# TensorE's program of the second attention, steps 24 to 55, as a loop of eight steps a turn

## The reference, cut to what matters

```python
x = x + tanh(g_xattn[0]) * attention0(layernorm(x), ctx)     # 8 heads of 64
x = x + tanh(g_ffn[0])   * experts(layernorm(x))             # 16 experts, the best 2 of each row
x = x + tanh(g_xattn[1]) * attention1(layernorm(x), ctx)     # 16 heads of 8
x = x + tanh(g_ffn[1])   * fp8_matmul(layernorm(x))
# attention1(q, c): Q = q@Wq+bq; K = c@Wk+bk; V = c@Wv+bv; softmax(Q K^T / sqrt(8)) V @ Wo + bo, by head
```

## Time and profile before

| | |
|---|---|
| time, median of 3 runs | 1152.83 us (1152.71 to 1156.85) |
| the profiled execution's time | 1153.63 us |
| its span, first to last instruction | 1151.9 us |
| PE, DVE, ACT, POOL busy | 90%, 71%, 51%, 56% of the span |
| stage C, VectorE's first to last instruction | 708.5 to 1149.5 us |
| mean granted clock of TensorE | 0.952 |

### The profile page before, as it was taken

How to read it: one execution, slowest core, us unless ns; L and a number is a source line. 1 busy time by engine, 2 the same in 40 slices (tenths; PEclk the granted TensorE clock), 3 DMA queues, 4 the chain that set the end, 5 groups by cost and what they waited for, 6 DMA issues and landing times. The chain is left out here.

```text
span 1151.9 us, 40516 instructions
## 1 busy us (share of the span) xinstructions
PE 1035.9 (90%) x13498; PEld 844.1 (73%) x13498; DVE 814.5 (71%) x2572; ACT 590.3 (51%) x1415; POOL 650.7 (56%) x1155
## 2 busy tenths in 40 slices
PE   4999999996999997499949996888999999899993
PEld 3787878774777775288848985666788888788882
DVE  1777777776777775655525555577899999799984
ACT  2666666662666564144515442234556555465554
POOL 1333333232777777566663545447777777577656
PEclk9999999997999999599979998799999999899997
DMA  3412112331334300144424543111111111111101
GB/s 76 90 42 52 42 38 61 91 75 40 92 95 108 98 25 27 55 139 140 134 74 130 144 137 89 30 30 29 32 38 37 32 37 38 30 37 34 33 24 31
DMA packets 106902, 74.39 MB, mean 65 GB/s; under 512 B 21360, under 2 KB 98288, under 8 KB 106736
## 3 DMA queue, kind: packets, MB, share of 16 engines
q1 hardware_dynamic: 98544, 55.40, 18.5%
q0 software_dynamic: 8192, 16.79, 4.9%
HBM read 38.60 MB, written 33.55 MB: 63 GB/s over the span
## 5 line engine op out<-in xcount | busy, mean ns | idle before, releaser
L678 ACT ACTIVATE arena<-PS 77x512 f32<-77x512 f32 (+4 forms) x736 | 303.9, 439 | 424.7 <-PE PS L1194 288.4
L1194 PE MATMUL PS<-arena 128*32 128x128 f32 (+5 forms) x9488 | 452.0, 292 | 36.6 <-DMA logit_bias<-in_bias 12.7
L1194 PEld LDWEIGHTS PS<-arena 128*32 128x32 f32 (+4 forms) x9488 | 352.5, 147 | 114.4 <-ACT arena L678 29.1
L604 POOL DMA_INDIRECT moe_in<-moe_results,slot x128 | 130.5, 1020 | 129.1 <-PE PS L1194 63.0
L1194 PE MATMUL PS<-w,arena 128*128 x960 | 192.4, 319 | 2.2 <-ACT arena L741 1.2
L524 POOL DMA_INDIRECT moe_rows<-arena x128 | 127.5, 996 | 71.8 <-POOL arena L520 50.3
L539 POOL TENSOR_TENSOR arena<-arena,minus_half 128x2 f32<-128x2 f32 (+1 forms) x70 | 47.5, 679 | 187.9 <-DVE arena L852 165.8
L1194 PEld LDWEIGHTS PS<-w,arena 128*128 128x128 f32 x960 | 135.0, 195 | 19.3 <-issue 6.2
L1075 DVE TENSOR_TENSOR arena<-PS,b_rows 128x256 f32<-128x256 f32 x160 | 67.7, 424 | 72.1 <-PE PS L1194 50.1
L1194 PEld LDWEIGHTS PS<-arena,wk_wq 128*128 128x128 f32 x512 | 80.3, 197 | 45.5 <-issue 43.0
L1087 DVE TENSOR_REDUCE arena<-PS 128x8 f32<-128x616 f32 x128 | 96.3, 794 | 18.4 <-PE PS L1194 13.1
(11 more groups left out here) (149 smaller groups left out, 1648.8 us busy)
## 6 DMA issues: line engine op xcount, KB each, us to landing
moe_rows<-zeros SPq DMA_DIRECT2D x64, 160.0 KB, 2.5
arena<-moe_rows SPq DMA_DIRECT2D x40, 256.0 KB
moe_results<-arena SPq DMA_DIRECT2D x40, 256.0 KB
residual<-in_x SPq DMA_DIRECT2D x64, 64.0 KB
w<-in_W SPq DMA_DIRECT2D x32, 128.0 KB
arena<-in_ctxC SPq DMA_DIRECT2D x64, 64.0 KB
out<-arena SPq DMA_DIRECT2D x64, 64.0 KB, 1.6
arena<-in_ctxT SPq DMA_DIRECT2D x32, 77.0 KB
```

The costliest lines, as they stand in the source:

```text
L604: g.indirect_dma_start(out=gathered(b, k), out_offset=None, in_=ys_flat[b // CB][:, :], in_offset=bass.IndirectOffsetOnAxis(ap=POS[k][:, b ...
L678: A.activation(o, i, ACT.Copy).then_inc(s[done], 1)
L1194: return T.matmul(o, l, r, start=start, stop=stop)
```

## The change

A span list of TensorE's own, `c_spans_of_tensor`, replaces the common one: steps 0 to 23 written out, steps 24 to 55 as a loop of 4 turns of 8 steps, steps 56 to 80 written out. The other engines keep `c_spans`.

```diff
+    LOOPC = 24
     TURN = 8
...
+        def c_spans_of_tensor():
+
+            return [(0, LOOPC, True), (LOOPC, NB - TURN, False), (NB - TURN, NB + LAST_LAG_C, True)]
...
-            for span in c_spans():
+            for span in c_spans_of_tensor():
                 run_steps(pe, NB, *span, step_c, TURN, LEADC)
```

## The result

The changed kernel takes 1178.20 us (median of 4 runs, 1175.31 to 1180.92), the kernel before 1154.84 (4 runs): a ratio of 1.0188, 95% interval 1.0165 to 1.0212. It is slower, as forecast, but by twice what was forecast: the measured time lies above my range of 1152 to 1171. That it is slower is clear of the noise; whether by more than 2% is not.

A forecast was written before the change was run, and what follows sets the result against it. Taken to be bound by a circle through PE and DVE, 5.99 us a step; 3 x 2.5 us of jump stalls plus 2 x 2.4 us of half clock, 12.3 us, gave 1165 us, range 1152 to 1171.

The forecast's parts named there:

- What bounds the kernel: Stage C: a circle through PE and DVE, 5.99 us a step, with 0.2 us of slack on PE before S1.
- The body isn't kept; each jump waits: TensorE's loop: some 2250 instructions are too many to keep, so all three jumps back wait for instructions; chance 0.60.
- the register instructions and the branch itself: TensorE's loop turns: 36 register instructions and one 213 ns branch a turn, both hidden behind queued matmuls, cost 0.
- The price of one such jump: a single stall of 3.2 us: Each jump back: 2.1 us load plus 1.1 us packet; less 0.5 covered and 0.2 slack, S1 is 2.5 us late.
- rival 3: Each jump back: a second wait of some 2 us for the next block, half clock always; 1173.5 us, chance 0.08.
- The clock: Behind the jumps: PE's clock falls to half after two of three, costing 2.4 us each.
- The sum: Three jumps at 2.5 us plus two half clocks at 2.4 us: 12.3 us more.
- 1 (the body is kept): At the jumps: the body stays with the engine, three 213 ns branches are hidden; 1152.8 us, chance 0.15.
- 4 (faster): GpSimd's pause near 994 us: may go if the body is kept and fetches fall, saving 5.4 us; 1147.4 us, chance 0.05.
- 2 (a short fetch): Each jump back: only 1.6 us, of which 0.9 reach S1, clock stays up; 1155.5 us, chance 0.12.

The follow-up runs named there:

- e5_pauses35: The written-out kernel before, with 35 waiting instructions as a TensorE pause at the start of steps 32, 40 and 48: 1160.99 us, ratio 1.0073.
- e1_turn4: The changed kernel with 4 steps a turn instead of 8, so 7 jumps back and a body of 1132 instructions: 1153.79 us, ratio 1.000.
- e3_shift36: The changed kernel with 36 instructions that only wait, put at the start of TensorE's program, moving the loop's start: 1165.86 us, ratio 1.0101.
- g1_two_jumps: The changed kernel with the loop over steps 24 to 47 only, so jumps at steps 32 and 40: 1171.29 us, ratio 1.0145.

## Why the prediction was wrong

**What bounds the kernel** was right: a circle through PE and DVE without slack. A pause of PE lengthened its step by at least as much: in e5_pauses35 pauses of 3.10 and 3.16 us made their steps 4.5 us longer.

**The body isn't kept; each jump waits** was right, though the trace of before couldn't decide it. The three pauses stand where I said, steps between them take 6.02 us, and the register instructions and the branch itself cost nothing that can be seen (e1_turn4).

**The price of one such jump: a single stall of 3.2 us** is the step that failed, by two things. The smaller one: the branch lasts 3.6 to 3.9 us, 1.5 us more in the three together. The 2.1 us of the smallest load and the 1.1 of a packet were its parts. At the first jump 1.03 us pass before the packet starts, it takes 1.20, and 1.34 more pass from its end to the end of the branch. The larger one: there are two stops a jump. I had this as rival 3, at 0.08 and 1173.5 us, with the condition "where less than half a block is left behind the target", and said that nothing speaks for or against. The condition could have been worked out: from the compiled program's length before the loop and q8's packets in the trace of before, which come at each 256th instruction, the target is 28 instructions ahead of a block's end. e3_shift36 shows what this is worth: 9.3 of the 23.6 us below.

**The clock** in two of three jumps, 2.4 us each, was too little. It fell in all three, and with two stops close together it stayed low for longer: 6.8, 13.7 and 6.8 us, against 3.4, 6.8 and 3.4 with the first stop alone (e3_shift36).

**The sum**: 3 x 2.5 + 2 x 2.4 = 12.3 us. Measured from the steps of the three jumps: 13.24 + 6.14, 13.33 + 8.31 and 12.67 + 5.99 for two steps each, less 12.04, are 7.3, 9.6 and 6.6, together 23.6 us. One thing worked the other way and wasn't in the sum: GpSimd's wait at step 48, worth 5.4 us before, now lies below the third jump. 23.6 - 5.4 is 18.2 of the 18.8 us that this part grew by. With one stop a jump, as I had summed it, e3_shift36's six steps grew by 15.3 us and not 12.3, and the same 5.4 were hidden. That its median, 1165.86, is all but the forecast of 1165 is luck.

**Rivals**: 1 (the body is kept) and 4 (faster) fell with the trace after; 2 (a short fetch) fell, no jump of the changed kernel is below 3.5 us. With a body that is kept GpSimd's pause stays (3.65 us in e1_turn4, at the same gather), so rival 4 had no ground: its condition came true there and its gain didn't.

## What to carry to other kernels

Before a loop is written for an engine, count its body in the compiled program: on TensorE here a body in 7 blocks of 256 instructions ran without a stall at its jumps, and bodies in 8 or more waited 3.3 to 4.0 us at every jump back. Where a long body can't be avoided, see that the jump's target lies at the start of a block, and take few long turns rather than many. A pause of TensorE of some 3 us in full work mostly cost more than it lasted, since the half clock followed. It didn't follow once, in g1_two_jumps, so take its price from several executions and not from one. Two stops close together cost more still.

## What the runs showed that I had not expected

- Where a body begins decides whether it is kept: 1741 instructions are kept from offset 8 in a block and not from offset 228.
- 36 instructions that do nothing, at the start of the program, made the looped kernel 9 us faster in its profile.
- GpSimd waits 3.45 us ahead of the gather of step 48 in every kernel here, looped or not, with its program moved or not; under TensorE's own pause it costs nothing.
- No version with a loop that gives the right result beats the kernel before: with the body kept (e1_turn4) it is the same within 0.2%.
- PE pauses of nearly equal length were followed by half clock for 3.4 us, for 6.8 us, and once not at all.
